# Token statistics of the next batches spread over four maxima in an attention score loop (Trainium2, one core)

## The chip, the cores and the metric

The kernel runs on one core of one Trainium2 chip. The metric is the device time of one launch in microseconds (us); the kernel before takes 1261.34 us, the median of three runs (1260.82 to 1265.86). The engines are called by their short names: PE is the matrix engine (TensorE), DVE the vector engine, ACT the scalar engine, POOL is GpSimd, and SP the engine that issues most of the DMAs.

## The reference, cut to what matters

The program is a small two-layer tower over 8 batches of 500 tokens with 128 features. A token embedding and a state-space layer come first, then a mixture of experts (`L0_ffn`), then the attention in which the change lies, then a second mixture of experts (`L1_ffn`). Every one of them reads a layer norm of the running activations `h`:

```python
h = h + _L0_ffn_ref(_layernorm(h, axis=-1), ...)
h = h + _L1_attn_ref(_layernorm(h, axis=-1), ...)
h = h + _L1_ffn_ref(_layernorm(h, axis=-1), ...)

def _layernorm(x, axis=-1, eps=1e-05):
    m = jnp.mean(x, axis=axis, keepdims=True)
    v = jnp.var(x, axis=axis, keepdims=True)
    return (x - m) / jnp.sqrt(v + eps)

# in _L1_attn_ref, H = 8 heads of dk = 16
QKs = jnp.einsum('bhle,bhse->bhls', q, K_sample) * scale
M = QKs.max(-1) - QKs.mean(-1)
U = jnp.argmax(M, axis=-1)
```

For each batch and head the attention needs, of every query token, the largest score over the keys. This is the bulk of its work: 8 batches, 8 heads, 500 x 500 scores each, of which only the row maxima are kept.

## The kernel before, in words

**Tiling.** The 500 tokens of a batch lie as J = 4 token tiles of R = 125 partitions; `h[:, t, :]` is tile t = 4b + j. The scores of a batch are made in 12 groups (`GROUPS`, line 35): for each of the four query tiles j, heads 0 to 2, 3 to 5, and 6 and 7. So the groups g = 0, 1, 3, 4, 6, 7, 9, 10 hold three heads and g = 2, 5, 8, 11 hold two.

**Two engines in turn.** PE makes a group's scores (`scores(b, g)`, lines 1890 to 1898; one 97-row bf16 matmul with 500 columns for each head, line 1896) into one of two sets of three PSUM banks. DVE takes the maxima of the group straight from those banks with one TENSOR_REDUCE (line 1330). PE waits for the maximum two groups back before it fills a set again (`scores_read`, line 1893), and DVE waits for `scores_filled` (line 1329).

**The front of the batch two ahead.** While batch b is scored, its own inputs having been made earlier, PE also makes the inputs of batch b + 2 in five pieces (`front`, lines 1870 to 1888), which stand in PE's program after the scores of g = 4, 5, 7, 8 and 10:

```python
for g in range(len(GROUPS)):
    scores(b, g)
    if b + 2 < B and g in (4, 5, 7, 8, 10):
        front(b + 2, (4, 5, 7, 8, 10).index(g))
```

Front 0 (line 1878) turns the four normalized token tiles of batch b + 2 and waits for them (`xa_ready`, line 1876). Front 1 (line 1881) makes the weighted mean of the tokens, front 2 (line 1884) its key, fronts 3 and 4 (line 1887) the queries and keys. PE works in the order of its program, so the scores of g = 5 come behind front 0.

**Where the normalized tokens come from.** DVE makes the statistics of the four tiles (`stats`, lines 961 to 967: four `bn_stats`, a settle, which is a wait for DVE's own earlier results, four `bn_aggr`), and `variance` (lines 969 to 974) settles again and raises `var_ready`. ACT takes the square root (`root`, line 1689). DVE then makes the reciprocal and the shift of the batch (`scales`, lines 976 to 981; L980 and L981) and raises `scales_ready`. ACT then normalizes the four tiles (`normalize`, line 1694) and raises `xa_ready`. In DVE's loop (lines 1326 to 1353) for b from 1 to 5 the whole `variance` of batch b + 2 stands behind the maximum of g = 0, and `scales` behind that of g = 2. For b = 0 the statistics were made before the loop, and `scales` stands behind g = 2. For b = 6 and 7 there is no batch two ahead.

**What else hangs on it.** Before the statistics of batch b + 2 DVE waits for `added`: POOL has by then added the last expert rows of that batch to `h` (line 915), after ACT weighted them (line 1789, in ACT's own loop behind front 2). ACT copies front 0 out (line 1776) and reads the means and keys (lines 1778 to 1781). From fronts 3 and 4 ACT and POOL make three bf16 parts (lines 1797, 1798, 1803, 891, 896). SP stores the normalized tokens (line 715) and the parts (line 701), and loads the parts as the `stack` of batch b + 2 (line 709), for which PE waits before that batch's first group.

Of the kernel before, what the change touches and what calls it, by code (L numbers as in the profile page):

```python
# [28 lines left out]
J = L // R  # L29
# [103 lines left out]
def tower_kernel(nc, a, out):  # L133
# [15 lines left out]
    with ExitStack() as ctx:  # L149
        sems = {}  # L150

        def S(name):
            if name not in sems:
                sems[name] = ctx.enter_context(nc.semaphore(name))
            return sems[name]

        def sb(name, shape, dt=F32):
            return ctx.enter_context(nc.sbuf_tensor(name, shape, dt))
# [9 lines left out]
        h = sb("h", [R, NT, D])  # L168
# [27 lines left out]
        bnst = sb("bnst", [R, 2 * J, 6])  # L196
        mv = sb("mv", [R, NT, 2])
# [756 lines left out]
        def _(dve):  # L954
            me = Steps(dve, S("dve_step"))
            v = nc.vector
# [4 lines left out]
            def stats(src, b, mean_var):  # L961

                for t in range(J * b, J * b + J):
                    me.did(v.bn_stats(bnst[:, t % (2 * J), :], src[:, t, :]))  # L964
                me.settle()
                for t in range(J * b, J * b + J):
                    me.did(v.bn_aggr(mean_var[:, t, :], bnst[:, t % (2 * J), :]))  # L967

            def variance(src, lo, hi):

                for b in range(lo, hi):
                    stats(src, b, mv)
                me.settle()
                dve.sem_inc(S("var_ready"), 1)

            def scales(n, lo, hi):

                w = slice(J * lo, J * hi)
                dve.wait_ge(S("root_ready"), n + 1)
                me.then(v.reciprocal(rs[:, w], rs[:, w]))  # L980
                v.scalar_tensor_tensor(shift[:, w], mv[:, w, 0], -1.0, rs[:, w], ALU.mult, ALU.mult).then_inc(S("scales_ready"), 1)  # L981
# [301 lines left out]
            def combine(c, b):  # L1283

                q = f"f{c.n}_"
                for i in range(J * c.K):
                    n = J * c.K * b + i
                    k, t = (i // J, J * b + i % J) if c.n == 0 else (i % c.K, J * b + i // c.K)
                    dve.wait_ge(S(f"got{n % 8}"), 16 * (8 * c.n + n // 8 + 1))
                    if k:  # L1290
                        dve.wait_ge(S(q + "combined"), n - J + 1 if c.n == 0 else n)
                    v.scalar_tensor_tensor(h[:, t, :], got[n % 8][0:R, :], gate[c.n][:, k, t:t + 1], h[:, t, :],
                                           ALU.mult, ALU.add).then_inc(S(q + "combined"), 1)
                dve.wait_ge(S(q + "combined"), c.K * J * (b + 1))
# [18 lines left out]
            def attention(me, dve):  # L1313

                for b in range(3):
                    combine(FFN[0], b)
                    variance(h, b, b + 1)
                    if b == 1:
                        dve.wait_ge(S("part1_ready"), 1)
                        TT(out=qk_rest, in0=qk_rest, in1=parts[:, :, 0, :], op=ALU.subtract).then_inc(S("rest_ready"), 1)  # L1320
                        dve.wait_ge(S("part2_ready"), 1)
                        dve.wait_ge(S("rest_ready"), 1)
                        TT(out=parts[:, :, 2, :], in0=qk_rest, in1=parts[:, :, 1, :], op=ALU.subtract).then_inc(S("parts_ready"), 1)
                    if b < 2:
                        scales(13 + b, b, b + 1)
                for b in range(B):
                    for g, (j, lo, hi) in enumerate(GROUPS):
                        n = len(GROUPS) * b + g
                        dve.wait_ge(S("scores_filled"), n + 1)
                        v.tensor_reduce(out=mcol[:, j, H * b + lo:H * b + hi], in_=ps[0:R, 3 * (n % 2):3 * (n % 2) + hi - lo, 0:L],  # L1330
                                        axis=AX.X, op=ALU.max).then_inc(S("scores_read"), 1)
                        if b + 2 < B:
                            if g == 0 and b:
                                dve.wait_ge(S("added"), 2 * b)
                                variance(h, b + 2, b + 3)
                            if g == 2:
                                scales(15 + b, b + 2, b + 3)
                        if n == LATE["MT"]:
                            pick(me, dve, 0)
                        if n == LATE["index"]:  # L1340
                            index(me, dve, 0)
                        if n == LATE["xsel"]:
                            take_xsel(dve, 0)
                        if n == LATE["qsel"]:
                            take_qsel(dve, 0)
                        if n == LATE["u"]:
                            take_u(dve, 0)
                        if n == LATE["ss"] + 2:
                            shift_scores(me, dve, 0)
                        if n == LATE["att"]:  # L1350
                            take_att(me, dve, 0)
                        if n == LATE["attT"]:
                            take_attT(dve, 0)
                tail(me, dve)
# [10 lines left out]
            def pick(me, dve, ph):  # L1365
                n = phase(ph)[1]

                def copy(p):
                    return v.tensor_copy(mrow[0:n, :], p[0:n, 0:L])
                take_piece(dve, "MT", ph, copy)  # L1370
                if ph == 0:
                    dve.wait_ge(S("front_read"), early("MT") + 1)
                else:
                    wait_evac(dve, "MT")
                me.then(v.max(m8[0:n, :], mrow[0:n, :]))

            def index(me, dve, ph):
                n = phase(ph)[1]
                me.then(v.max_index(i8[0:n, :], m8[0:n, :], mrow[0:n, :]))
                me.then(v.tensor_copy(i8f[0:n, :], i8[0:n, 0:1]))  # L1380
                TS(chosen[0:n, :], i8f[0:n, :], batch_row[0:n, :], float(L * PHASES[ph][0]), ALU.add, ALU.add).then_inc(S("chosen_ready"), 1)

            def take_xsel(dve, ph):
                lo, n = phase(ph)
                take_piece(dve, "xsel", ph, lambda p: v.tensor_copy(xsel[:, lo:lo + n], p[:, 0:n]))

            def take_qsel(dve, ph):
                lo, n = phase(ph)
                take_piece(dve, "qsel", ph, lambda p: v.scalar_tensor_tensor(
                    qsel[:, lo:lo + n].rearrange("p (b h) -> p b h", h=H), p[:, 0:n].rearrange("p (b h) -> p b h", h=H),  # L1390
                    bcol[:, 0:1], own8.unsqueeze(1).broadcast_to([128, n // H, H]), ALU.add, ALU.mult))

            def take_u(dve, ph):
                lo, n = phase(ph)
                first = uz.offset + (72 if ph == 0 else 64) * PHASES[ph][0]
                take_piece(dve, "u", ph, lambda p: v.tensor_copy(
                    bass.AP(tensor=uz.tensor, offset=first, ap=[list(uz.ap[0]), [72, n // H], [1, H]]),
                    p[:, 0:n].rearrange("p (b h) -> p b h", h=H)))

            def shift_scores(me, dve, ph):  # L1400
                n = phase(ph)[1]
                if ph == 0:
                    dve.wait_ge(S("front_filled"), early("ss") + 1)
                    p = early_bank("ss")
                else:
                    wait_bank(dve, "ss")
                    p = bank(at["ss", 0])
                me.then(v.tensor_reduce(out=nmx[0:n, :], in_=p[0:n, 0:L], axis=AX.X, op=ALU.max))
                TS(nmx[0:n, :], nmx[0:n, :], -SCALE, None, ALU.mult).then_inc(S("nmx_ready"), 1)

            def take_att(me, dve, ph):
                n = phase(ph)[1]
                if ph == 0:
                    dve.wait_ge(S("front_read"), early("ss") + 1)
                else:
                    wait_evac(dve, "ss")
                me.then(v.reciprocal(asum[0:n, :], asum[0:n, :]))
                TS(att[0:n, :], att[0:n, :], asum[0:n, :], None, ALU.mult).then_inc(S("att_ready"), 1)
# [187 lines left out]
            for b in range(B):  # L1606
                wait_bank(dve, "z", b)
                pz = bank(at["z", b])[0:R, :].rearrange("p (j d) -> p j d", j=J)
                for j in range(J):
                    t = J * b + j  # L1610
# [604 lines left out]
```

## Time and profile before

| | before |
|---|---|
| median of three runs | 1261.34 us |
| lowest, highest | 1260.82, 1265.86 us |
| span of the profiled execution, first to last instruction | 1254.4 us |
| mean granted TensorE clock | 0.721 of full speed |
| DVE busy | 748.9 us (60%) |
| PE busy | 737.2 us (59%) |
| maxima (L1330), x96 | 143.7 us busy, 470.2 to 663 us |

The profiled execution's own time is given only as its span, 1254.4 us; the median run is 6.9 us above that. The score loop fills the span from 470 to 663 us, 15% of it. A timeline row gives the start, the length in us, engine, line, operation, output <- input and the number of instructions merged into the row; in brackets stands the engine's idle time before the row and what ended it. A DVE row's length runs to the end of its last instruction; instructions of DVE overlap in the record by some 0.08 us. The chain of waits goes backward from the last event of a stretch and says at each step what held it. The granted clock is given as a share of 2.4 GHz, so 0.50 is 1.2 GHz.

### The profile page before, as it was taken

How to read it: one execution, taken by the hardware profiler on the slowest of the kernel's cores; microseconds unless marked ns; L12 is line 12 of the kernel's file. 1: busy time of each engine (PE TensorE's matmuls, PEld its weight loads, DVE VectorE, ACT ScalarE, POOL GpSimd, SP SyncE). 2: the span in 40 equal slices, each digit the busy share in tenths (PEclk: the TensorE clock that was granted, in tenths of full speed). 3: DMA queues.
4: the chain of work that ended last, by engine and by line, in shares of the span. 5: the costliest groups of instructions: out<-in, count | busy, mean ns of one | idle time of the engine just before them, and what ended most of it. 6: DMA issues, size and time to landing. Idle time of an engine off the chain costs nothing.

```text
span 1254.4 us, 16064 instructions
## 1 busy us (share of the span) xinstructions
PE 737.2 (59%) x4622; PEld 585.6 (47%) x4622; DVE 748.9 (60%) x2175; ACT 406.2 (32%) x1123; POOL 536.2 (43%) x562
## 2 busy tenths in 40 slices
PE   0205966669999237878597413577777894452000
PEld 0205355559999214434255401366666894442000
DVE  6896174856666318788776799555555552275222
ACT  2274151524444133433102306533333462220000
POOL 8853000245450645563100005756666306347664
PEclk9657975559999656676665655589999997665555
DMA  2390049502221266657500404033333222112221
GB/s 67 113 388 1 1 143 320 173 24 68 71 72 42 58 119 127 142 124 137 94 0 1 129 0 138 23 83 85 88 86 88 77 64 66 53 43 77 63 54 52
DMA packets 113503, 111.45 MB, mean 89 GB/s; under 512 B 15891, under 2 KB 99922, under 8 KB 113170
## 3 DMA queue, kind: packets, MB, share of 16 engines
q1 hardware_dynamic: 100172, 83.36, 24.5%
q0 software_dynamic: 13248, 27.06, 8.4%
q8 instruction: 42, 0.69, 0.2%
q14 instruction: 41, 0.34, 0.1%
HBM read 76.08 MB, written 34.26 MB: 88 GB/s over the span
## 4 chain that ended last, share of the span: by engine, by line
PE 46%; DVE 30%; issue 10%; another core or an unknown queue 6%; ACT 3%; DMA 2%; POOL 1%; SPq 1%; DVEq 0%; ACTq 0%; POOLq 0%
PE ps L639 13%; PE ps L646 12%; DVE wide L1330 6%; DVE h L1309 5%; PE ps L1896 4%; PE ps L634 2%; DVE bnst L964 2%; DVE wide L1208 2%; PE ps L2066 2%; PE ps L2107 2%; PE ps L2156 1%; ACT wide L1694 1%; PE ps L2046 1%; DVE mv L967 1%
## 5 line engine op out<-in xcount | busy, mean ns | idle before, releaser
L871 POOL DMA_INDIRECT wide<-xrows,holder x188 | 180.1, 958 | 137.5 <-PE ps L634 91.1
L639 PE MATMUL ps<-wide 128*128 (+1 forms) x1324 | 205.9, 288 | 42.6 <-issue 25.4
L646 PE MATMUL ps<-big,wide 128*128 x1312 | 196.2, 282 | 40.3 <-issue 21.7
L639 PEld LDWEIGHTS ps<-wide 128*128 128x128 f32 x1324 | 174.7, 198 | 56.2 <-issue 53.3
L646 PEld LDWEIGHTS ps<-big,wide 128*128 128x128 f32 x1312 | 171.8, 196 | 43.7 <-issue 43.6
L512 DVE TENSOR_SCALAR wide<-ps,wide 128x128 f32<-128x128 f32 x331 | 109.2, 348 | 129.5 <-PE ps L639 78.6
L1330 DVE TENSOR_REDUCE wide<-ps 125x3 f32<-125x1500 f32 (+1 forms) x96 | 143.7, 1540 | 46.4 <-PE ps L1896 44.4
L606 ACT ACTIVATE wide<-ps,wide 128x128 f32<-128x128 f32 x331 | 114.0, 366 | 169.8 <-PE ps L639 132.9
L1896 PE MATMUL ps<-big 97*125 97x500 bf16 x256 | 105.4, 548 | 40.3 <-DVE wide L1330 33.0
L949 POOL DMA_INDIRECT wide<-results,place x96 | 95.8, 998 | 68.2 <-SPq L494 26.8
L862 POOL TENSOR_SCALAR wide<-tileno,sm 125x128 f16<-125x128 f16 x64 | 40.8, 644 | 168.4 <-DVE sm L1195 143.9
L624 ACT COPY wide<-ps 128x128 f32<-128x128 f32 x258 | 68.4, 265 | 114.9 <-PE ps L646 82.2
L507 DVE COPY wide<-ps 128x128 f32 x184 | 53.4, 290 | 80.2 <-PE ps L634 67.6
L504 DVE COPY wide<-big 128x258 f32 (+2 forms) x264 | 87.0, 330 | 3.9 <-issue 3.8
L905 POOL DMA_INDIRECT wide<-results,place x64 | 61.0, 954 | 60.6 <-SPq L494 34.3
L1896 PEld LDWEIGHTS ps<-big 97*125 97x125 bf16 x256 | 42.9, 193 | 88.6 <-DVE wide L1330 51.2
L2156 PE MATMUL ps<-b,cst 8*125 8x128 f32 (+1 forms) x128 | 33.0, 435 | 75.4 <-issue 70.5
L1309 DVE SCALAR_TENSOR_TENSOR h<-wide,big,h 125x128 f32<-125x128 f32 x96 | 32.7, 351 | 74.6 <-DVE h L1309 24.7
L2156 PEld LDWEIGHTS ps<-b,cst 8*125 8x125 f32 (+1 forms) x128 | 28.3, 322 | 81.3 <-issue 72.3
L2046 PE MATMUL ps<-cst,wide 125*128 125x125 f32 x96 | 22.4, 390 | 62.8 <-ACT wide L1694 62.7
L634 PE MATMUL ps<-cst,wide 128*128 128x128 f32 x188 | 53.4, 285 | 7.2 <-DMA wide<-xrows,holder 4.6
L884 POOL DMA_INDIRECT big<-results,place x32 | 30.4, 950 | 58.5 <-DMA results<-wide 49.1
(384 smaller groups left out, 1197.2 us busy)
## 6 DMA issues: line engine op xcount, KB each, us to landing
results<-wide SPq DMA_DIRECT2D x129, 128.0 KB, 1.8
big<-kappa SPq DMA_DIRECT2D x8, 1750.0 KB, 21.4
big<-parts SPq DMA_DIRECT2D x96, 125.0 KB
big<-in_L_ffn_W_dram SPq DMA_DIRECT2D x10, 1024.0 KB, 9.6
big<-in_L_ffn_W_dram SPq DMA_DIRECT2D x64, 128.0 KB, 2.7
parts<-wide SPq DMA_DIRECT2D x24, 250.0 KB
xrows<-wide SPq DMA_DIRECT2D x2, 1792.0 KB
wide<-xrows,holder POOLq DMA_INDIRECT x188
```

What stands on the lines that cost most here:

```text
L504: v.tensor_copy(ring.w1[u % U], w1v[:, bass.ds(w1, c.wcols)]).then_inc(S(p + "w1_ready"), 1)
L512: last = v.tensor_scalar(ring.hid[u % 2][:, 128 * k:128 * k + 128], ps[:, 4 + u % 2, 128 * k:128 * k + 128], w[:, hid + k:hid + k + 1], 0. ...
L606: last = s.activation(ring.hid[u % 2][:, 128 * k:128 * k + 128], ps[:, 2 + u % 2, 128 * k:128 * k + 128], ACT.Relu, bias=w[:, hid + k:hid ...
L634: t.transpose(ps[:, u % 2, 0:128], ring.rows[u % RING], ident).then_inc(S(p + "turned"), 1)
L639: last = t.matmul(ps[:, (2 if k < c.HC // 2 else 4) + u % 2, 128 * k:128 * k + 128], ring.w1[u % U][:, 128 * k:128 * k + 128], turned, sta ...
L646: last = t.matmul(ps[:, 6 + u % 2, 0:D], ring.hid[u % 2][:, 128 * k:128 * k + 128], w[:, D * k:D * k + D], start=k == 0, stop=k == c.HC - 1)
L871: gp.indirect_dma_start(ring.rows[j % RING], None, xrows[:, :], bass.IndirectOffsetOnAxis(ap=holder[:, j:j + 1], axis=0)).then_inc(S(f"row ...
L949: gp.indirect_dma_start(got[m % 8], None, results[f][:, :], bass.IndirectOffsetOnAxis(ap=place[f][:, k, t:t + 1], axis=0)).then_inc(S(f"go ...
L1309: v.scalar_tensor_tensor(h[:, t, :], rows[0:R, :], swapped_gate[:, k, t:t + 1], h[:, t, :], ALU.mult, ALU.add).then_inc(S("f1_combined"), 1)
L1330: v.tensor_reduce(out=mcol[:, j, H * b + lo:H * b + hi], in_=ps[0:R, 3 * (n % 2):3 * (n % 2) + hi - lo, 0:L], axis=AX.X, op=ALU.max).then_ ...
L1896: last = t.matmul(ps[0:R, 3 * (n % 2) + head - lo, 0:L], stack[0:SROWS, 0, b % 2, head, R * j:R * j + R], stack[0:SROWS, 1, b % 2, head, : ...
L2156: last = t.matmul(p[0:R, D * j:D * j + D], cT[0:c.E, R * j:R * j + R], b2[0:c.E, f, :], start=True, stop=True)
```

## The change

For b from 1 to 5, the statistics of batch b + 2 are no longer made in one run behind the maximum of g = 0. Behind g = 0 stands one `bn_stats` (tile 0). Behind g = 1, 2 and 3 stands one `bn_stats` each (tiles 1, 2, 3), a settle, and the `bn_aggr` of the tile before. Behind g = 3 come besides a second settle and the `bn_aggr` of tile 3, which itself raises `var_ready`. `scales` of that batch stands behind the maximum of g = 4, no longer behind that of g = 2. For b = 0 it stays behind g = 2. The wait for `added` stays behind g = 0. PE, ACT, POOL and SP run the programs they ran.

```diff
                         if b + 2 < B:
                             if g == 0 and b:
                                 dve.wait_ge(S("added"), 2 * b)
-                                variance(h, b + 2, b + 3)
-                            if g == 2:
+                            if b and g < J:
+                                t = J * (b + 2) + g
+                                me.did(v.bn_stats(bnst[:, t % (2 * J), :], h[:, t, :]))
+                                if g:
+                                    me.settle()
+                                    me.did(v.bn_aggr(mv[:, t - 1, :], bnst[:, (t - 1) % (2 * J), :]))
+                                if g == J - 1:
+                                    me.settle()
+                                    v.bn_aggr(mv[:, t, :], bnst[:, t % (2 * J), :]).then_inc(S("var_ready"), 1)
+                            if g == (4 if b else 2):
                                 scales(15 + b, b + 2, b + 3)
```

## Rows read from the trace of the kernel before

**Rows 1.** The page: share of the chain that ended last, by engine

```profile
PE 46%; DVE 30%; issue 10%; another core or an unknown queue 6%; ACT 3%; DMA 2%; POOL 1%; SPq 1%; DVEq 0%; ACTq 0%; POOLq 0%
```

**Rows 2.** Busy time by window, one batch each, statistics to statistics

```profile
core 0: us, PE busy (x) PEld busy (x) DVE busy (x) ACT busy (x) POOL busy (x), PEclk, DMA share, GB/s
493.38:516.33 22.95, 18.22 (x50) 10.19 (x50) 19.30 (x23) 8.74 (x23) 13.92 (x12) 0.63 0.67 136
516.33:539.09 22.76, 17.21 (x50) 9.53 (x50) 19.31 (x23) 10.19 (x23) 15.20 (x13) 0.70 0.63 136
```

**Rows 3.** Timeline of DVE, batch b = 2 of the score loop

```profile
516.33 0.86 DVE L964 BATCH_NORM_STATS2 bnst<-h 125x6 f32<-125x128 f32 x4
517.23 0.38 DVE L967 BATCH_NORM_AGGREGATE mv<-bnst 125x2 f32<-125x6 f32 x4
517.75 2.83 DVE L1330 TENSOR_REDUCE wide<-ps 125x3 f32<-125x1500 f32 x2
519.39 1.19 DVE L1330 TENSOR_REDUCE wide<-ps 125x2 f32<-125x1000 f32 x1
520.50 0.17 DVE L980 RECIPROCAL rs<-rs 125x4 f32<-125x4 f32 x1
520.70 0.16 DVE L981 SCALAR_TENSOR_TENSOR shift<-mv,rs 125x4 f32<-125x4 f32 x1
521.08 3.35 DVE L1330 TENSOR_REDUCE wide<-ps 125x3 f32<-125x1500 f32 x2 [0.22 <-PE ps L1896]
522.71 1.71 DVE L1330 TENSOR_REDUCE wide<-ps 125x3 f32<-125x1500 f32 x1
524.62 1.20 DVE L1330 TENSOR_REDUCE wide<-ps 125x2 f32<-125x1000 f32 x1 [0.20 <-issue]
527.47 4.45 DVE L1330 TENSOR_REDUCE wide<-ps 125x3 f32<-125x1500 f32 x3 [1.65 <-PE ps L1896]
533.09 6.08 DVE L1330 TENSOR_REDUCE wide<-ps 125x3 f32<-125x1500 f32 x4 [1.17 <-PE ps L1896]
```

**Rows 4.** The chain of waits, the same batch

```profile
517.70 0.30 ACT rs L1689
518.00 2.90 issue
520.90 1.66 ACT wide L1694 x4
522.55 0.14 issue
522.69 1.06 PE ps L1878 x4
523.75 0.83 PE ps L1896 x2
524.59 1.50 PE ps L1881 x8
526.08 1.36 PE ps L1896 x3
```

**Rows 5.** Timeline of PE, the same batch

```profile
519.53 2.76 PE L1896 MATMUL ps<-big 97*125 97x500 bf16 x6 [2.42 <-DVE wide L1330]
530.13 1.88 PE L1887 MATMUL ps<-wide,big 128*128 128x500 f32 x2
533.53 1.00 PE L1887 MATMUL ps<-wide,big 128*128 128x500 f32 x2
534.87 0.64 PE L1896 MATMUL ps<-big 97*125 97x500 bf16 x2 [0.34 <-DVE wide L1330]
537.60 0.85 PE L1896 MATMUL ps<-big 97*125 97x500 bf16 x3 [0.19 <-DVE wide L1330]
```

**Rows 6.** Groups by line, 493 to 608 us, the five batches b = 1 to 5

```profile
L980 DVE RECIPROCAL rs<-rs 125x4 f32<-125x4 f32 x5 | 0.8, 166 | 0.0
```

**Rows 7.** PE alone by window: us, PE busy (x), PEclk, DMA share, GB/s

```profile
518.00:532.00 14.00, 11.73 (x33) 0.54 0.92 187
532.00:539.00 7.00, 4.84 (x17) 0.95 0.22 66
539.00:556.00 17.00, 13.79 (x38) 0.52 0.80 159
```

**Rows 8.** Timeline of POOL and SP, b = 2 and 3

```profile
530.92 2.67 POOL L915 TENSOR_TENSOR h<-wide,h 125x512 f32<-125x512 f32 x2 [5.30 <-ACT wide L1789]
543.05 6.33 SPq L709 DMA_DIRECT2D big<-parts  x6
```

## Prediction

> **What bounds the kernel now.** I began with the page. Its chain that ended last is spread over PE and DVE [rows 1], so no single engine bounds the whole kernel, and what the change is worth must be read in its own stretch. I therefore cut the score loop into windows of one batch [rows 2]. A batch lasts 22.76 to 22.95 us (five such batches, b = 1 to 5). DVE is busy for 19.3 us of it and PE for 17.2 to 18.2 us. Both are high and neither is full: the two engines hand work to each other, and it is the order of the hand-overs that sets the batch.
>
> The timeline of DVE shows where they bite [rows 3]. Behind the maximum of g = 0 comes the run of statistics: it starts at 516.33 and the next maximum (g = 1) at 517.75, so the run costs 1.42 us. The maxima of g = 1 and 2 follow, then `scales` at 520.50, then g = 3 and 4 at 521.08 and 522.71, and g = 5 at 524.62. From the start of the statistics to the start of g = 5 it is 8.29 us. In this stretch DVE stands idle only twice, for 0.22 and 0.20 us; its larger idle times, 1.65 before g = 6 and 1.17 before g = 9, come later, behind pieces of the front.
>
> The chain of waits shows what was nearly late at g = 5 [rows 4]. ACT takes the root at 517.70 and then stands for 2.90 us; that is `scales` being behind g = 2 on DVE. Shift ends at 520.86 [rows 3], ACT normalizes from 520.90 for 1.66 us, PE begins front 0 at 522.69, and 1.93 us later (524.62) DVE can begin g = 5, whose scores stand behind front 0 in PE's program. So PE's front 0 already starts the moment the tokens come, 0.14 us after them: there is **no slack between `scales` and the maximum of g = 5**. That is the fact on which the prediction rests.
>
> **The change part by part.**
>
> *The statistics in four pieces.* The instructions are the same 4 + 4, with more settles among them. A `bn_stats` alone lasts 0.28 us, and four in a row 0.86 [rows 3], which is 0.20 from one to the next. Behind g = 0 I count 0.20. A settle makes the next instruction start 0.04 us after the end of the one before it (516.33 + 0.86 = 517.19, then 517.23) where unsettled ones overlap by 0.08; a `bn_aggr` lasts 0.15. Behind g = 1 and g = 2 I count 0.28 + 0.04 + 0.15, less 0.05 for overlap, = 0.42 each; behind g = 3, with the second settle and the second `bn_aggr`, 0.60. The sum is 1.64 against 1.42 for the run. The bounds: 1.42, if settles between other work cost nothing, and 2.20, if each of the four pieces ends with the 0.14 us that lies between the last `bn_aggr` (517.61) and the maximum at 517.75. I take 1.64, since it is built from the single steps.
>
> The Trainium skill says in "VectorE: DVE Perf Modes", section "The DRAIN you can't avoid", that a semaphore between two DVE instructions costs nothing extra, as the pipeline empties either way. By that rule the pieces would cost what the run costs, and my sum would be 1.1 us lower over five batches. The row above speaks against it by 0.12 us a settle (0.04 after the end against 0.08 before it).
>
> *What the earlier maxima gain.* `scales` leaves the place between g = 2 and 3. There DVE waited 0.22 us for PE as well, so the step from g = 2 to 3 was 1.69 us (519.39 to 521.08) where a two-head maximum alone takes 1.11 (519.39 to 520.50). I count back from the stats' start, 516.33: g = 1 starts at 516.53; g = 2 at 516.53 + 1.64 + 0.42 = 518.59; g = 3 at 518.59 + 1.11 + 0.42 = 520.12; g = 4 at 520.12 + 1.63 + 0.60 = 522.35. That is 0.36 before the 522.71 of now. PE does not hold these up: the scores of g = 3 took from 519.53 to the maximum at 521.08, 1.55 us [rows 3, 5], and would now be released at 518.25 by g = 1, so they are there at 519.80, 0.32 us before they are wanted. Those of g = 4 come 1.4 us after that at the latest. If that cover were gone, the step would fall back to what PE gives, some 0.2 us a batch.
>
> *`scales` behind g = 4.* DVE is through with g = 4 at 522.35 + 1.64 = 523.99, and the shift ends 0.36 us later at 524.35. The root is no obstacle: `var_ready` comes behind g = 3 at 522.35, and ACT has the 1.64 us of g = 4 for a root of 0.30 us [rows 4]; ACT is idle there now (the 2.90 us). ACT begins to normalize at 524.39 and ends at 526.04, front 0 begins at 526.18, and g = 5 at 526.18 + 1.93 = 528.11. Now it is 524.62. **Each batch gets 3.49 us longer.** Queued behind the waiting front 0 on PE are the scores of g = 5 and all after; DVE waits for these and has nothing else: with everything scored up to g = 4 and both sets of banks read, PE stands idle for about 4.8 us and DVE for about 3.8.
>
> *From g = 5 on* everything hangs on front 0 at the distances of now: g = 6 starts 2.85 us after g = 5 (scores behind front 1, 1.50 us [rows 4]), and so on to the next g = 0. I cost this part at nothing. The other queues move with it. POOL's add ends at 533.59 and the statistics that wait for it come at 539.09 [rows 3, 8]; both lie behind front 2, so these 5.5 us stay. SP's `xattn` store waits for `xa_ready`, and the stores of parts behind it wait for fronts 3 and 4, later still, so SP loses nothing. Its last loads of the `stack` for batch 4 are issued by 549.38 [rows 8]; batch 4's first scores come some 3 us before its statistics, which start at 539.09 + 22.9 = 562.0, so there are 9.6 us now, and 3.49 more with the change.
>
> *The sum.* The batches b = 1 to 5 are five [rows 6]; b = 0, 6 and 7 keep their order. 5 x 3.49 = 17.4 us. Against the profiled span: 1254.4 + 17.4 = 1271.8 us. The median run lies 6.9 us above the span (1261.34 against 1254.4), which stays: 1278.8 us. With the bounds of the pieces, 5 x 3.27 = 16.3 and 5 x 4.05 = 20.3, it is 1277.7 to 1281.6. What comes after the loop starts from its end, and nothing there is waiting for a clock of its own that I could find, so I pass the whole sum through.
>
> **The rivals.**
>
> *The clock makes up for it (no change, not slower).* PE has 1.2 GHz (0.52 to 0.54 granted) through the front and nearly 2.4 (0.95) from front 3 to the statistics [rows 7]; it falls after the statistics have kept it idle for 2.42 us [rows 5]. The change takes this gap away. If the high clock then lasted through fronts 0 to 3, these would shrink: front 0 and the scores of g = 5, 1.93 us, to 0.43 + 0.64 = 1.1; front 1 and the scores of g = 6, 2.86, to 0.75 + 0.82 = 1.6; and the 1.17 us before g = 9 would go, as front 3 took 1.88 us low and front 4 1.00 high [rows 3 to 5]. This gives back 3.25 of 3.49 us a batch: 1262.5 us. It decides from the point at which the high clock outlasts front 0. Against it: PE would still stand 4.8 us before front 0, twice the gap that preceded the fall now. Chance 0.05.
>
> The Trainium skill's "TensorE: Matmul & The Clock Gate", section "Why this matters for your kernels", says that idle gaps between bursts of matmuls bring the clock back to half. By the gap removed alone this rule is for the rival and 1262.5 us; by the gap added it is for my sum. That the clock falls after the idle 2.42 us agrees with it.
>
> *The normalized tokens are hidden after all (no change).* If front 0's start were not tied to `scales` as the chain shows, only DVE's own order would count, and a batch would change by -0.36 to +0.22 us: 1259.5 to 1262.4. For it speaks only that PE's own idle rows before front 0 are small; against it, that front 0 follows ACT by 0.14 us. Chance 0.03. Both rivals together would make the kernel faster: 5 x (0.36 + 3.25) = 18 us off, 1243.3 us. Chance 0.02.
>
> *The clock stays low longer (slower still).* With 4.8 us more of idle PE in a batch, the rise now at 532 may come a batch's half later. Then front 4 takes 1.9 instead of 1.0 us, and the pairs and threes behind it 1.04 and 1.4 instead of 0.64 and 0.85; as DVE covers most of these, I put 0.7 to 1 us a batch: 1282.3 to 1283.8. Chance 0.08.
>
> **How the numbers follow.** The forecast, 1278.8 us, has 0.82. The range runs from 1272, a part of the clock's gain (1.3 us a batch), to 1285, the low clock with the dear pieces. It leaves out the three cases of no slowdown, 0.10. Within 0.5% (6.3 us, about what a measurement here can tell from no change) lie the first two rivals, 0.08; faster 0.02; slower 0.82 + 0.08 = 0.90.
>
> **What would show it.** Right, if in the changed profile: `scales` stands behind g = 4 and ACT begins to normalize within 0.1 us of it; PE waits 4 to 5 us before each of the five L1878 rows, with ACT L1694 as what ended it; DVE stands 3.5 to 4 us idle before g = 5; a batch lasts 26.2 to 26.5 us; g = 5 to the next g = 0 takes what it takes now; and the loop's end moves by 17 us. The first step is wrong if a piece costs over 0.6 us. The sum is wrong if the granted clock is near 1 at front 0, or if another piece (the stack, `added`) ends a wait that nothing ended before.

## The result, and the profile after

The changed kernel takes 1278.99 us (median of four runs, 1273.29 to 1279.17) against 1262.16 us for the kernel before (four runs): a ratio of 1.0133, 95% interval 1.0107 to 1.0158. It is slower, by 16.8 us (13.5 to 19.9 by the interval); forecast were 17.4 us and 1278.8 us. The profiled run of the changed kernel took 1278.94 us, its span is 1277.2 us.

First the timeline of DVE in the changed kernel, for the batch b = 2 of the score loop (line numbers after 1343 are eight higher than before: L1904 is the scores' line 1896, L1886 the line 1878 of front 0, L1702 the line 1694).

```profile
519.19 0.28 DVE L1337 BATCH_NORM_STATS2 bnst<-h 125x6 f32<-125x128 f32 x1
519.39 1.70 DVE L1330 TENSOR_REDUCE wide<-ps 125x3 f32<-125x1500 f32 x1
521.01 0.28 DVE L1337 BATCH_NORM_STATS2 bnst<-h 125x6 f32<-125x128 f32 x1
521.32 0.18 DVE L1340 BATCH_NORM_AGGREGATE mv<-bnst 125x2 f32<-125x6 f32 x1
521.42 1.17 DVE L1330 TENSOR_REDUCE wide<-ps 125x2 f32<-125x1000 f32 x1
522.50 0.28 DVE L1337 BATCH_NORM_STATS2 bnst<-h 125x6 f32<-125x128 f32 x1
...
522.92 1.69 DVE L1330 TENSOR_REDUCE wide<-ps 125x3 f32<-125x1500 f32 x1
524.52 0.28 DVE L1337 BATCH_NORM_STATS2 bnst<-h 125x6 f32<-125x128 f32 x1
...
525.16 1.69 DVE L1330 TENSOR_REDUCE wide<-ps 125x3 f32<-125x1500 f32 x1
526.76 0.17 DVE L980 RECIPROCAL rs<-rs 125x4 f32<-125x4 f32 x1
526.96 0.17 DVE L981 SCALAR_TENSOR_TENSOR shift<-mv,rs 125x4 f32<-125x4 f32 x1
530.90 1.20 DVE L1330 TENSOR_REDUCE wide<-ps 125x2 f32<-125x1000 f32 x1 [3.77 <-PE ps L1904]
533.75 4.45 DVE L1330 TENSOR_REDUCE wide<-ps 125x3 f32<-125x1500 f32 x3 [1.65 <-PE ps L1904]
539.58 6.08 DVE L1330 TENSOR_REDUCE wide<-ps 125x3 f32<-125x1500 f32 x4 [1.37 <-PE ps L1904]
```

It answers to [rows 3]. The pieces cost 0.20 (519.19 to 519.39), 0.41, 0.42 and 0.64 us: 1.67 in all, where the run cost 1.42. The maximum of g = 4 starts 5.97 us after the start of the statistics, where it was 6.38. Then the shift ends, and DVE stands idle for 3.77 us: the new wait. From g = 5 on the distances are nearly as they were: 2.85 us to g = 6 as before, and 5.83 from there to g = 9, where it was 5.62 in the batch of [rows 3] and 5.82 in three of the four others (as 504.52 to 510.34). From the statistics to g = 5 it is 11.71 us, where it was 8.29.

The chain of waits for the same stretch, answering to [rows 4], has the whole wait as "issue": the profile names nothing that ended it. The second listing shows ACT in the same batch, the third shows PE at front 0 two batches later:

```profile
521.14 3.00 PE ps L1904 x6
524.15 4.82 issue
528.96 1.07 PE ps L1886 x4
530.03 0.83 PE ps L1904 x2
```

```profile
525.28 0.30 ACT L1697 ACTIVATE rs<-mv,alpha 125x4 f32<-125x4 f32 x1 [5.67 <-DVE mv L1343]
527.17 1.65 ACT L1702 ACTIVATE wide<-h,shift,rs 125x128 f32<-125x128 f32 x4 [1.60 <-issue]
```

```profile
581.39 1.07 PE L1886 MATMUL ps<-cst,wide 125*128 125x125 f32 x4 [4.80 <-ACT wide L1702]
```

The shift ends at 527.13, ACT begins at 527.17 and ends at 528.82, front 0 begins 0.14 us later. PE stood 4.80 to 4.82 us before front 0 in each of the five batches, and in four of them the profile names ACT's normalize as what ended it.

The windows of one batch, statistics to statistics, answer to [rows 2] (columns as there):

```profile
492.82:519.19 26.37, 17.99 (x50) 9.74 (x50) 19.41 (x24) 8.79 (x22) 13.84 (x13) 0.61 0.53 118
519.19:545.57 26.38, 18.35 (x50) 10.03 (x50) 19.42 (x23) 8.74 (x23) 13.83 (x13) 0.61 0.55 117
545.57:571.63 26.06, 16.87 (x50) 9.18 (x50) 19.42 (x24) 9.95 (x23) 15.04 (x13) 0.67 0.56 119
```

Busy times stay (DVE 19.4, PE 17 to 18); only the batch is longer, by 3.1 to 3.6 us. From the first statistics to the end of the run of maxima behind them, the five batches take 133.2 us (492.82 to 626.00) where they took 115.8 (493.38 to 609.19): **17.4 us more**. The loop as a whole, from the start of its first maximum to that of its last, grew from 191.7 (470.21 to 661.95) to 210.4 us (469.66 to 680.04), 18.6. The other 1.3 are in batches 6 and 7, where DVE waits 5.36 instead of 4.74 us for PE's gathered rows and 1.94 instead of 1.28 a little later. The change is not needed for that: together these two waits are 6.0 us before and 7.3 after, and in the twelve kernels below 5.5 to 7.6, with 5.7 in the first of them, whose scales are as late. The two spans differ by 22.8 us, and the 4.2 beyond the loop lie within the scatter of what no kernel here changes: the time outside the loop (span less loop) was 1062.7 us before and 1066.8 after, and in the twelve kernels below it lay anywhere from 1059.1 to 1070.8. The loop's length is therefore given with each experiment. It comes from one trace of each kernel, and the two waits in batches 6 and 7 alone move it by up to 2 us.

### The profile page after: what moved, and what is told of

The parts are those of the page before. It is cut to its first block, busy times and chain, and to the rows that moved or that the text cites. A ratio compares the mean times of both kernels' runs of the same rounds, so it can differ in the third digit from the quotient of the medians.

```text
span 1277.2 us, 16059 instructions
## 1 busy us (share of the span) xinstructions
PE 736.7 (58%) x4622; PEld 584.5 (46%) x4622; DVE 750.0 (59%) x2175; ACT 405.4 (32%) x1123; POOL 535.6 (42%) x562
## 4 chain that ended last, share of the span: by engine, by line
PE 45%; DVE 31%; issue 11%; another core or an unknown queue 4%; ACT 4%; DMA 3%; SPq 1%; POOL 0%; DVEq 0%; ACTq 0%; POOLq 0%
PE ps L639 13%; PE ps L646 11%; DVE wide L1330 7%; DVE h L1309 4%; PE ps L1904 4%; PE ps L634 3%; DVE wide L1208 2%; PE ps L2074 2%; PE ps L2115 2%; DVE bnst L964 2%; PE ps L2164 2%; ACT wide L1702 2%; PE ps L2054 1%; PE ps L2011 1%
## 5 line engine op out<-in xcount | busy, mean ns | idle before, releaser
L1904 PE MATMUL ps<-big 97*125 97x500 bf16 x256 | 105.7, 545 | 35.1 <-DVE wide L1330 27.0
L1904 PEld LDWEIGHTS ps<-big 97*125 97x125 bf16 x256 | 42.0, 191 | 85.6 <-DVE wide L1330 46.0
```

The source lines that it names most:

```text
L1904: last = t.matmul(ps[0:R, 3 * (n % 2) + head - lo, 0:L], stack[0:SROWS, 0, b % 2, head, R * j:R * j + R], stack[0:SROWS, 1, b % 2, head, : ...
```

## The experiments

The theory: the cost comes from the scales alone, as front 0 stands in PE's program between the scores of g = 4 and g = 5. The rivals: the pieces with their settles cost the time; the granted clock decides; late scales cost wherever front 0 stands. The kernels of a group ran on one chip with the kernel before among them.

**Scales late, statistics in one run.** On the kernel before:

```diff
-                            if g == 2:
+                            if g == (4 if b else 2):
                                 scales(15 + b, b + 2, b + 3)
```

> The statistics stay in one run behind g = 0; only the scales move, from behind g = 2 to behind g = 4, for b = 1 to 5. Theory (late scales are the whole cost, through front 0): g = 3 and 4 start as in the kernel before (521.08, 522.71 in its second such batch), the shift ends 0.36 us after g = 4 at 524.71, normalize and front 0 add 0.04 + 1.65 + 0.14 and g = 5 comes 1.93 later at 528.47, so 3.85 us more a batch, 19 us in all, about 1281.4 us: slower than the changed kernel by 2 us. Rival (the pieces with their settles are what costs): the time goes back to about 1262.

1273.78 us against 1257.85 for the kernel before on that chip: 1.0155 (1.0109 to 1.0202). The loop took 210.8 us, 19.1 more than before, which is the expected 19.

```profile
528.00 0.16 DVE L981 SCALAR_TENSOR_TENSOR shift<-mv,rs 125x4 f32<-125x4 f32 x1
528.20 1.65 ACT L1694 ACTIVATE wide<-h,shift,rs 125x128 f32<-125x128 f32 x4 [6.74 <-issue]
529.99 1.07 PE L1878 MATMUL ps<-cst,wide 125*128 125x125 f32 x4 [4.24 <-ACT wide L1694]
531.93 1.20 DVE L1330 TENSOR_REDUCE wide<-ps 125x2 f32<-125x1000 f32 x1 [3.77 <-PE ps L1896]
```

The timeline shows the same 3.77 us before g = 5 without a single piece. The pieces are not what costs; beside the late scales they even save something. The five batches, measured as above, took 135.3 us here and 133.2 in the changed kernel, 2.1 less, which is the expected 2. (The whole loops differ by only 0.5 us, as batches 6 and 7 went the other way. The two ratios, 1.0155 and 1.0133, lie within each other's intervals.)

**Pieces, scales early.** On the changed kernel, tiles 2g and 2g + 1 behind g = 0 and 1, and the scales back behind g = 2:

```diff
-                            if b and g < J:
-                                t = J * (b + 2) + g
+                            for i in (2 * g, 2 * g + 1) if b and g < 2 else ():
+                                t = J * (b + 2) + i
...
-                            if g == (4 if b else 2):
+                            if g == 2:
                                 scales(15 + b, b + 2, b + 3)
```

> The statistics in pieces with their settles, but tiles 0 and 1 behind g = 0 and tiles 2 and 3 behind g = 1, and the scales behind g = 2 where they were. Theory: the shift ends within 0.1 us of where it ended before, so the time is that of the kernel before, 1262 us within 1.5. Rival (the pieces cost): 1270 or more, near the 1279 of the changed kernel.

1256.2 us, 0.9991 (0.9975 to 1.0008); loop 192.2 us against 191.7. The pieces alone change nothing that a run here can tell, and with the run before this settles which part of the change costs.

**Scales one maximum sooner.** The changed kernel with `if g == (3 if b else 2)`.

> The changed kernel with the scales behind g = 3 instead of g = 4, right behind the last aggregate. Theory (each us by which the shift comes later is a us of the batch): DVE now stands some 0.45 us for ACT's root, the shift ends about 1.2 us earlier than in the changed kernel, and the kernel is 5 x 1.2 = 6 us faster than it, about 1273 us, still 11 us slower than before. Rival (only the order of scales against the scores of g = 5 matters, not the time): same as the changed kernel, 1279. Rival (the pieces cost): 1279 too.

1265.41 us, 1.0070 (1.0034 to 1.0106); loop 202.7 us, 7.7 less than in the changed kernel and 11.0 more than before. (By time it is 7.6 us more than before, 4.3 to 13.3 by the interval, where 11 was expected.)

```profile
523.95 0.18 DVE L1343 BATCH_NORM_AGGREGATE mv<-bnst 125x2 f32<-125x6 f32 x1
524.50 0.18 DVE L980 RECIPROCAL rs<-rs 125x4 f32<-125x4 f32 x1 [0.36 <-ACT rs L1697]
524.71 0.16 DVE L981 SCALAR_TENSOR_TENSOR shift<-mv,rs 125x4 f32<-125x4 f32 x1
524.79 1.71 DVE L1330 TENSOR_REDUCE wide<-ps 125x3 f32<-125x1500 f32 x1
528.63 1.20 DVE L1330 TENSOR_REDUCE wide<-ps 125x2 f32<-125x1000 f32 x1 [2.13 <-PE ps L1904]
```

DVE stands 0.36 us for ACT's root, and the whole is still cheaper: from the start of the statistics (518.08) the shift ends at 6.79 instead of 7.94 us, 1.15 earlier, and g = 5 starts at 10.55 instead of 11.71, 1.16 earlier. A microsecond of `scales` is a microsecond of the batch. (Five times that is 5.8 us; the five batches gave 6.1, and the rest of the loop's 7.7 is in batches 6 and 7.)

**PE kept busy in its wait.** The changed kernel with eight matmuls ahead of the wait, whose result the transposes overwrite (`b` is here the batch made ahead, so `b > 2` are the five changed batches):

```diff
                     if i == 0:
+                        for head in range(8) if b > 2 else ():
+                            t.matmul(p[0:R, 0:L], stack[0:SROWS, 0, b % 2, head, 0:R], stack[0:SROWS, 1, b % 2, head, :], start=True, stop=True)
                         pe.wait_ge(S("xa_ready"), b + 1)
```

> The changed kernel with eight idle score matmuls (500 columns, their result is overwritten) put on PE ahead of its wait before front 0, for b = 1 to 5. Theory: PE stands there for 4.8 us, eight take 3.3 us at 1.2 GHz, so they cost nothing: 1279 us, if the clock stays low through the front. Rival of the clock: if the added work raises the granted clock from 0.5 to near 1 at front 0, the steps from front 0 to g = 5 and to g = 6 shrink from 1.93 and 2.85 towards 1.1 and 1.6 and the idle time before g = 9 goes, 3.2 us a batch, and the time falls towards 1263 us with the stall before front 0 unchanged.

1271.1 us, 1.0117 (1.0081 to 1.0152); loop 208.5 us, 1.9 less than the changed kernel, with the five batches 2.3 less. The timeline of PE at two of the five places:

```profile
524.31 3.04 PE L1885 MATMUL ps<-big 97*125 97x500 bf16 x8
529.22 0.65 PE L1888 MATMUL ps<-cst,wide 125*128 125x125 f32 x4 [1.87 <-ACT wide L1702]
529.71 0.63 PE L1906 MATMUL ps<-big 97*125 97x500 bf16 x2
...
576.12 3.54 PE L1885 MATMUL ps<-big 97*125 97x500 bf16 x8
581.04 1.10 PE L1888 MATMUL ps<-cst,wide 125*128 125x125 f32 x4 [1.38 <-issue]
581.93 1.04 PE L1906 MATMUL ps<-big 97*125 97x500 bf16 x2
```

At the first the clock had risen by front 0 (granted 1.00 from 527 to 530; front 0 took 0.65 us instead of 1.07, and DVE's wait before g = 5 was 2.89 instead of 3.77), and it was low again in front 1 (0.56, then 0.50). At the second it stayed at 0.50. It had risen at two of the five places. So the added work did give back some 0.9 us at each of these two, and cost nothing that shows at the other three (DVE's wait was 3.70 us there); the 16 us of the clock's rival were not to be had this way.

**Four orders of the front.** If PE's order sets the batch, it should be open to a gain as well. In all four, the line of the front was changed on the kernel before, as here in the first; the second and third also have the scales behind g = 1, and the fourth has the first's order, the scales behind g = 1 and the statistics behind g = 11 of the batch before.

```diff
-                        if b + 2 < B and g in (4, 5, 7, 8, 10):
-                            front(b + 2, (4, 5, 7, 8, 10).index(g))
+                        if b + 2 < B and g in (4, 7, 8, 10, 11):
+                            front(b + 2, (4, 7, 8, 10, 11).index(g))
```

> The kernel before, statistics and scales where they were, but the pieces of the front stand on PE behind g = 4, 7, 8, 10, 11 instead of 4, 5, 7, 8, 10. Theory (the batch is set by the order of hand-overs on PE): the idle time of DVE before g = 6 (1.65 us, scores behind front 1) and before g = 9 (1.17 to 1.37, behind front 3) shrinks, as front 1 and front 3 now stand behind maxima of 1.63 us; about 1.5 to 2 us less a batch in six batches, 9 to 12 us: 0.991 to 0.993 of before. Rival (the clock takes it back): with PE's dense stretch loosened the granted clock rises later or not at all and the time stays, 0.998 to 1.002.

> Front behind g = 4, 7, 8, 9, 10, and the scales behind g = 1 instead of 2. Theory: the normalized tokens come 1.1 us sooner, so front 0 no longer waits, and the idle times before g = 6 and 9 shrink; fronts 3 and 4 now press on g = 10 and 11. 1.3 to 1.8 us a batch, 0.991 to 0.994 of before. Rival of the clock as in the run before: 0.998 to 1.002.

> Front behind g = 4, 7, 9, 10, 11 and the scales behind g = 1. Theory: of the four orders this leaves DVE the least idle time from g = 4 to 11, some 2 us less a batch, 0.990 of before. Rival: front 2 comes two maxima later, so the added rows of the next batch (5.5 us early in the kernel before) come about 2 us early or late for the statistics behind g = 0, and the stack two maxima later; a wait for one of them would take 1 to 3 us a batch back, 1.00 of before.

> The statistics in one run behind g = 11 of the batch before instead of g = 0, scales behind g = 1, front behind 4, 7, 8, 10, 11. Theory: the tokens are normalized before PE wants them, as in the two runs before, and the statistics lie where PE has fronts 3 and 4 to do, so 1.5 to 2.5 us less a batch, 0.988 to 0.993. Rival: the added rows are not there at g = 11 (they came 5.5 us before the statistics, and a maximum and its place take 1.6, front 2 is later by 1.6), which would cost up to 1 us a batch: 0.995.

The kernel before took 1261.8 us here. Order 4, 7, 8, 10, 11: 1255.96 us, 0.9955 (0.9934 to 0.9976), loop 185.6 us. Order 4, 7, 8, 9, 10 with scales behind g = 1: 1256.11 us, 0.9964 (0.9938 to 0.9990), loop 187.5. Order 4, 7, 9, 10, 11 with scales behind g = 1: 1261.21 us, 1.0008 (0.9988 to 1.0028), loop 193.6. Statistics behind g = 11: 1258.68 us, 0.9976 (0.9959 to 0.9993), loop 188.0. The first gave 6.1 us of loop, less than the 9 to 12 expected; the others, which were to be better, were worse. The third kernel's timelines of DVE and of POOL show something that none of the expectations had:

```profile
543.40 1.76 DVE L981 SCALAR_TENSOR_TENSOR shift<-mv,rs 125x4 f32<-125x4 f32 x1
...
543.05 2.08 POOL L896 TENSOR_TENSOR wide<-wide 128x1000 bf16<-128x1000 f32 x1
```

The shift, 0.16 us long in the kernel before, takes 1.76 us, and ends (545.16) 0.03 us after POOL's add (545.13). By the line's own view its five instances took 1.13 to 1.76 us there, 1.52 to 1.76 with the statistics behind g = 11, and 0.16 to 1.23 in the other two. With the scales behind g = 1, or with PE's later part moved, the shift falls into POOL's add of the third part. In the third kernel DVE also waits for ACT's root (0.98 us at most), which stands behind ACT's own cast of the parts before. Added up over its five batches, the shifts are 6.6 us longer than 0.16 each, where they are 2.1 us longer in the first kernel, and the two waits for the root are 1.8 us. That is 6.3 of the 8.0 us by which its loop is longer than the first one's. No run takes the hold away and keeps the order, so this cause is read from the rows and not shown by a run. DVE stood idle before none of the statistics, so the added rows, the rival named for it, were not waited for.

**The changed kernel with front 0 out of the way.** On the changed kernel, the front behind g = 6, 7, 8, 10, 11:

> The changed kernel (four pieces, scales behind g = 4), but with the front behind g = 6, 7, 8, 10, 11 instead of 4, 5, 7, 8, 10. Theory (the late scales cost only because front 0 stands between the scores of g = 4 and g = 5): the scores of g = 5 and 6 no longer stand behind the normalized tokens, DVE's idle 3.76 us before g = 5 goes, and of the 17 us most come back: within 0.5% of before. What may remain is a crowd of fronts 0 to 2 between g = 6 and 9, up to 1.2 us a batch, so 1.000 to 1.005 of before. Rival (late scales cost wherever front 0 stands, since parts and stack come later too): 1.01 of before or more.

1256.42 us against 1257.46: 0.9996 (0.9977 to 1.0015); loop 193.7 us, 16.6 less than in the changed kernel. The shift is as late as in the changed kernel, 7.94 us after the start of the statistics (517.53):

```profile
525.31 0.16 DVE L981 SCALAR_TENSOR_TENSOR shift<-mv,rs 125x4 f32<-125x4 f32 x1
525.39 1.19 DVE L1330 TENSOR_REDUCE wide<-ps 125x2 f32<-125x1000 f32 x1
526.80 1.72 DVE L1330 TENSOR_REDUCE wide<-ps 125x3 f32<-125x1500 f32 x1 [0.21 <-issue]
529.65 1.72 DVE L1330 TENSOR_REDUCE wide<-ps 125x3 f32<-125x1500 f32 x1 [1.14 <-PE ps L1904]
```

The maximum of g = 5 now follows the shift at once; the 3.77 us are gone, with the statistics and the scales of the change untouched. So those 3.77 us came from the scores that stood behind the waiting front 0 on PE, and not from the pieces or from the late scales as such. It does not show that the late scales now cost nothing. Front 0 still begins 0.14 us after the tokens, and PE stands 0.54 us before it. All five pieces of the front stand in other places here, which is worth something by itself: with front 0 left behind g = 4, the order 4, 7, 8, 10, 11 took 6.1 us off the loop. The run that would tell, this order with early scales, was not made; the nearest one, with front 0 one place sooner and early scales (the second of the next three), has a loop 10.9 us shorter.

**Front 0 one maximum later, three ways.** On the kernel before, order 5, 7, 8, 10, 11 (front 0 one place later than in the order 4, 7, 8, 10, 11, and all five pieces later than in the kernel before); the same with the two-tile pieces from above; the same with the scales behind g = 3.

> The kernel before with the front behind g = 5, 7, 8, 10, 11. Against the order 4, 7, 8, 10, 11 only front 0 moves, by one maximum, so PE no longer stands 0.86 us for the normalized tokens behind g = 4. Theory: as that order or up to 0.4 us a batch better, 0.993 to 0.996 of before. Rival: nothing gained by it, as what PE saves at g = 5 it needs at g = 6: 0.995 to 0.997.

> The same order of the front (5, 7, 8, 10, 11) with the statistics in pieces of two tiles behind g = 0 and 1 and the scales behind g = 2. Theory: the scores of g = 3 are released 0.9 us sooner than behind the whole run, PE's 2.42 us of idle time there is cut, and DVE's 0.2 us before g = 3 with it; 0 to 0.3 us a batch better than the same order with the run: 0.992 to 0.996. Rival: DVE is the bound there and the pieces only add settles: same or 0.1% slower than with the run.

> The order 5, 7, 8, 10, 11 with the scales behind g = 3. In the two orders before, the shift (two inputs from SBUF) ended 0.03 us after POOL's add of the third part in each case and took 0.63 to 1.76 us instead of 0.16. Theory: behind g = 3 the shift comes 1.6 us later, past POOL's add, and takes 0.16 again, which gives DVE 0.5 us a batch; front 0 then waits up to 1 us for the tokens, but has a maximum in hand: 0.993 to 0.997. Rival: the wait at front 0 costs what the shift gives, 0.998 to 1.002.

1247.05, 1246.95 and 1255.16 us against 1257.46: 0.9928 (0.9903 to 0.9954), 0.9928 (0.9903 to 0.9954) and 0.9995 (0.9977 to 1.0013). The loops took 182.9, 182.9 and 190.4 us against 191.7. **The first beats both kernels by an edit of one line:**

```profile
516.34 0.16 DVE L981 SCALAR_TENSOR_TENSOR shift<-mv,rs 125x4 f32<-125x4 f32 x1
516.54 4.45 DVE L1330 TENSOR_REDUCE wide<-ps 125x3 f32<-125x1500 f32 x3
521.53 7.77 DVE L1330 TENSOR_REDUCE wide<-ps 125x3 f32<-125x1500 f32 x5 [0.53 <-issue]
529.66 1.20 DVE L1330 TENSOR_REDUCE wide<-ps 125x2 f32<-125x1000 f32 x1 [0.36 <-PE ps L1896]
531.13 1.72 DVE L1330 TENSOR_REDUCE wide<-ps 125x3 f32<-125x1500 f32 x1 [0.28 <-PE ps L1896]
```

Of 3.2 us of DVE's idle time in a batch before [rows 3] 1.2 are left, and the batch lasts 20.8 us (511.98 to 532.77) where it lasted 22.8. This is the best of the batches, and the clock has a part in it, as the windows of this batch and the next show (columns as in [rows 2]):

```profile
511.98:532.77 20.79, 15.58 (x50) 8.09 (x50) 19.37 (x23) 9.35 (x22) 13.69 (x13) 0.75 0.73 146
532.77:555.51 22.74, 18.39 (x50) 10.19 (x50) 19.90 (x23) 9.10 (x22) 14.91 (x13) 0.62 0.62 140
```

With the clock at 0.62 the batch lasts 22.7 us, 0.2 less than before at 0.63 (22.95); with 0.75, more than in any of the first four batches before (0.63 to 0.70), it lasts 20.8. The expectations had the clock only as a rival that takes the gain back. Here it came with the gain, and no run tells which of the two, the shorter waits or the higher clock, brought the other. The pieces again change nothing. In the third the shift takes 0.16 us each time, as expected, but front 0 waits for the tokens:

```profile
521.29 1.07 PE L1878 MATMUL ps<-cst,wide 125*128 125x125 f32 x4 [0.96 <-ACT wide L1694]
```

and DVE stands 1.45 us before g = 6. The rival of that run held in its number. Its premise did not: the expectation took the long shift from the orders before, while in the first of these three kernels it took 0.16 us in four of five batches (0.66 in the other), so there was little to win. Against that kernel the loop is 7.5 us longer. At an equal clock a batch is only 0.4 to 0.6 us longer (23.32 us at 0.63 against 22.74 at 0.62; 21.75 at 0.69 against 21.38 at 0.68); the rest goes with the clock, whose mean is higher in the first kernel.

## Why the prediction was right

The mechanism was right, and the sum over the five batches as well. That the two medians, 1278.8 forecast and 1278.99 measured, agree to 0.2 us is luck: the measured difference is known only to some 3 us, the loop grew by 18.6, and the sum's other step was off, for the span came to 1277.2 us where the sum had 1271.8. The 6.9 us that the prediction carried from span to median are no fixed distance; the changed kernel's profiled run lies 1.7 us above its own span.

*No slack between scales and g = 5*: held in each of the five batches, and shown from three sides (late scales alone: +19.1 us of loop; scales sooner by 1.15: g = 5 sooner by 1.16; the front moved: the wait before g = 5 gone).

*The pieces at 1.64 us*: they took 1.67. The bounds 1.42 and 2.20 were not needed. Two terms within a piece were off and cancelled: a `bn_aggr` with a settle before it lasts 0.18 us, not 0.15, and the overlap behind it is 0.08, not 0.05. The trace bears out the price of a settle: `bn_aggr` starts 0.03 us after the end of `bn_stats` (521.29, 521.32), where unsettled work overlaps by 0.08.

*The shift at 8.02 after the statistics, g = 5 at 11.78*: 7.94 and 11.71. Step by step the 3.49 us a batch were 3.42, and 3.1 to 3.6 as the clock's rise fell sooner or later before g = 9 (1.05 or 1.37 us of idle time there). The sum over the five, 17.4 us, was 17.4 by the profile.

*DVE idle for about 3.8 us and PE for about 4.8*: 3.77 and 4.82. A batch was to last 26.2 to 26.5 us; three of those measured took 26.37 or 26.38, one 26.06.

*Nothing else waits*: right as far as the runs tell. In batches 6 and 7, for which I had counted nothing, the profile of the changed kernel has 1.3 us more, at the gathered rows; the run with late scales alone has 0.3 us less there than the kernel before, so this is scatter and not the change. POOL's add ends at 539.87 and the statistics start at 545.57: the 5.5 us of margin are 5.7.

*The clock's rival* fell, and its premise with it. I had tied the fall of the clock to PE's 2.42 us of idle time behind the statistics. The change removed that gap, and the clock fell in the same place of the program all the same, ahead of the scores of g = 3, and stayed at 0.50 until after 540 us, past fronts 0 to 3. The windows of PE alone in the changed kernel show the fall (us, PE busy, PEclk, DMA share, GB/s):

```profile
515.00:517.00 2.00, 0.92 (x5) 1.00 0.23 66
517.00:519.00 2.00, 1.35 (x6) 1.00 0.39 132
519.00:521.00 2.00, 0.64 (x2) 0.94 0.30 89
521.00:523.00 2.00, 1.86 (x4) 0.50 0.97 232
```

From 515 to 521 PE was never idle for more than 1.2 us, but it was busy for only 2.9 of 6 us; the fall lies in an idle stretch of 1.18 us (519.96 to 521.14). So the removed gap was not what the fall hung on: a thin stretch with short gaps was followed by it too. The Trainium skill ("TensorE: Matmul & The Clock Gate", section "Why this matters for your kernels") warns of idle gaps between bursts of matmuls, and of longer ones than the 2.42 us before or the 1.18 us here; so the page does not speak of either fall, and the agreement that the prediction found goes further than the page.

## What to carry to other kernels

Before moving a step that another engine waits for, follow it to the end of the chain and ask what stands behind the waiter in that engine's program: here 0.36 us of arithmetic put off by two maxima held up PE for 4.8 us, because a piece with nothing to do with the next scores stood before them. The cure is on the waiter's side as much as on the producer's: with early scales, the order with all five pieces later gave 0.7%, of which front 0's own place is worth about 2.7 us of loop (185.6 us with it behind g = 4, 182.9 behind g = 5, one trace of each, the clock's part in it unknown); and with front 0 two places later the late scales no longer stopped the next scores, though the kernel was no faster than before. Spreading a 1.4 us run over its neighbours was worth nothing in itself here, where its engine is busy on both sides of it.

## What the runs showed of the hardware

A DVE instruction with two inputs from SBUF can be held by POOL: the shift on 125 x 4 elements took 0.16 us alone and up to 1.76 us when it started inside POOL's 2.08 us TENSOR_TENSOR, and ended 0.01 to 0.04 us after it (seventeen such shifts in five of the kernels), while the reciprocal before it, with one input, kept its 0.17 to 0.18 us inside the same instruction. It is not held by all that POOL does: in the changed kernel the shift at 526.96 ran inside a DMA_INDIRECT of POOL (526.95 to 527.89) and took 0.17 us; shifts that started inside one took 0.16 or 0.17 us in eleven of the kernels and 0.20 in the twelfth. The Trainium skill names the contention ("GPSIMD Engine Reference", section "Key points": the engine shares its SBUF interfaces with VectorE, in contention with DVE instructions that have two SBUF inputs); for the TENSOR_TENSOR the trace agrees. Where a short step lies in time against POOL's long ones is thus part of its price.
